# Three subtractions moved in an attention kernel: one within VectorE's order, two from VectorE to GpSimd

## The reference: a cross-attention transformer block

```python
h = _layernorm(x, ln1_g, ln1_b)
x = _attention(h, h, sa_wq, sa_wk, sa_wv, sa_wo, sa_bo) + x
h = _layernorm(x, ln2_g, ln2_b)
x = _attention(h, cond_emb, ca_wq, ca_wk, ca_wv, ca_wo, ca_bo) + x
h = _layernorm(x, ln3_g, ln3_b)
p = h @ ff_w1 + ff_b1
a, gate = (p[..., :D_FF], p[..., D_FF:])
h = a * jax.nn.gelu(gate, approximate=False) @ ff_w2 + ff_b2
return h + x
```

## Time and profile before

| what | before |
|---|---|
| median of three runs | 2842.57 us (2842.28 to 2843.34) |
| the profiled execution, its own time | 2842.41 us |
| its span in the profile | 2840.6 us |
| TensorE busy (matmul) | 2796.0 us, 98% |
| VectorE busy | 2262.0 us, 80% |
| ScalarE busy | 1910.5 us, 67% |
| GpSimd busy | 1468.7 us, 52% |

### The profile page before, as it was taken

One profiled execution on the slowest core, in us unless ns is written; L12 is line 12 of the kernel. 1 busy time (PEld: TensorE's weight loads), 2 busy tenths in 40 slices (PEclk: granted clock), 3 DMA queues, 4 the chain that ended last, 5 costly groups with the idle time before them and its releaser, 6 DMA issues.

```text
span 2840.6 us, 72796 instructions
## 1 busy us (share of the span) xinstructions
PE 2796.0 (98%) x25278; PEld 2490.1 (88%) x25278; DVE 2262.0 (80%) x3494; ACT 1910.5 (67%) x6043; POOL 1468.7 (52%) x1311
## 2 busy tenths in 40 slices
PE   8999999999999999999999999999999999999999
PEld 7888888888888888888888888888888889999999
DVE  7888888888888888888888888888888865555554
ACT  6777777777777777877777777777777754444443
POOL 5444444444444444755555555555555564554554
PEclk9999999999999999999999999999999999999999
DMA  6666666666666666767777776666666642222222
GB/s 158 151 160 161 162 161 162 162 154 153 155 153 153 151 153 153 179 166 173 172 173 172 171 171 164 164 164 164 165 164 163 149 101 86 80 74 82 84 74 64
DMA packets 355330, 413.33 MB, mean 146 GB/s; under 512 B 122017, under 2 KB 209441, under 8 KB 355233
## 3 DMA queue, kind: packets, MB, share of 16 engines
q1 hardware_dynamic: 345088, 395.29, 57.2%
q10 hardware_dynamic: 10144, 16.78, 1.6%
HBM read 94.52 MB, written 49.02 MB: 51 GB/s over the span
## 4 chain that ended last, share of the span: by engine, by line
PE 58%; issue 17%; POOL 12%; DVE 11%; ACT 1%; POOLq 0%; DMA 0%; DVEq 0%; ACTq 0%
PE unit_ps L629 31%; PE s_ps L629 12%; POOL probs L1357 10%; PE unit_ps L653 8%; PE s_ps L641 7%; DVE neg_max L1107 3%; DVE blocks L1121 2%; DVE hT_lo L1145 2%; DVE qk L1132 1%; POOL x_rb L1344 1%; ACT probs L911 1%; DVE row_blocks L1098 1%; POOL rstd L1336 1%; DVE a_lo L1127 0%; DVE hT_lo L1149 0%
## 5 line engine op out<-in xcount | busy, mean ns | idle before, releaser
L1357 POOL TENSOR_TENSOR probs<-probs,row_inv 128x1024 f32<-128x1024 f32 x512 | 972.6, 1900 | 1076.5 <-DVE row_inv L1112 1076.4
L911 ACT ACTIVATE probs<-s_ps,neg_max 128x256 f32<-128x256 f32 x2048 | 950.2, 486 | 508.7 <-DVE neg_max L1107 507.7
L1121 DVE STREAM_TRANSPOSE blocks<-probs 128x1024 f32<-128x1024 f32 x512 | 633.2, 1237 | 194.6 <-POOL probs L1357 194.6
L1107 DVE TENSOR_REDUCE neg_max<-s_ps 128x4 f32<-128x1024 f32 x512 | 611.5, 1195 | 5.6 <-PE s_ps L641 2.7
L629 PE MATMUL unit_ps<-hT_hi,w_hi 128*128 128x256 f32 x2048 | 580.0, 287 | 5.6 <-DVE hT_lo L1145 3.1
L629 PE MATMUL unit_ps<-hT_hi,w_lo 128*128 128x256 f32 x2048 | 555.1, 277 | 0.0
L629 PE MATMUL unit_ps<-hT_lo,w_hi 128*128 128x256 f32 x1792 | 497.3, 278 | 0.0
L653 PE MATMUL unit_ps<-pT,v_f 128*64 128x256 f32 x4096 | 456.6, 381 | 0.2 <-issue 0.2
L911 ACT ACTIVATION_READ_ACCUMULATOR probs<-s_ps,neg_max 128x1 f32 x2048 | 442.0, 216 | 0.0
L641 PEld LDWEIGHTS s_ps<-qk 64*128 64x128 f32 x6144 | 374.9, 185 | 70.6 <-issue 42.0
L641 PE MATMUL s_ps<-qk 64*128 64x256 f32 x6144 | 426.6, 284 | 5.9 <-ACT probs L911 5.4
(11 more groups left out here) (76 smaller groups left out, 4866.0 us busy)
## 6 DMA issues: line engine op xcount, KB each, us to landing
pT<-blocks SPq DMA_DIRECT2D x1024, 256.0 KB, 4.5
rows_t_dram<-row_blocks SPq DMA_DIRECT2D x91, 256.0 KB, 2.2
rows_in<-rows_t_dram SPq DMA_DIRECT2D x91, 256.0 KB, 4.4
x_res<-in_x_dram SPq DMA_DIRECT2D x32, 256.0 KB, 3.1
x_sa_dram<-x_out SPq DMA_DIRECT2D x32, 256.0 KB, 2.2
x_ln<-x_sa_dram ACTq DMA_DIRECT2D x32, 256.0 KB, 4.9
ctx_in<-in_ctx_dram SPq DMA_DIRECT2D x32, 256.0 KB, 4.1
x_res<-x_sa_dram SPq DMA_DIRECT2D x32, 256.0 KB, 2.8
```

The lines of the kernel that those rows point to most:

```text
L911: op = nc.scalar.activation(probs[:, m % 2, r, :].rearrange("p (j b c) -> p j b c", j=IT, c=BLK), scored.rearrange("p (j c b) -> p j b c", ...
L1107: nc.vector.tensor_reduce(neg_max[:, m % RING, :], s_ps[:, m % 2, :, :].rearrange("p h (i j) -> p (h i) j", j=S), AX_X, ALU.max, negate=Tr ...
L1121: nc.vector.transpose(blocks[:, n % 2, :, m % 2, :].rearrange("p b (j r c) -> p r j b c", j=IT, c=BLK), probs[:, m % 2, :, :].rearrange("p ...
L1357: nc.gpsimd.tensor_tensor(probs[:, m % 2, :, :], probs[:, m % 2, :, :], row_inv[:, m % RING, :].unsqueeze(2).broadcast_to([P, ROWS, S]), A ...
```

## The change

Three subtractions move; none is added or dropped.

1. VectorE's `attended_lo(t - 1, 3)`, the remainder of the fourth product with v, stood in step 2 behind the inverted sums of pair 4. It now stands behind the first maximum of the step (pair 4), ahead of the transpose of pair 3. This holds in self and in cross attention.
2. In cross attention, `x_remainder(t + 1)` leaves VectorE and is done by GpSimd, in step 2 behind the multiply of pair 5. In self attention it stays on VectorE in step 3.
3. `context_remainder(t + 1)` leaves VectorE's step 3 and is done by GpSimd, behind the rows' remainder and ahead of the 64x256 context subtraction that GpSimd had already.

```diff
-            def context_remainder(b):
-                dve.wait_ge(at.ctx_hi, b - ca.first + 1)
-                nc.vector.tensor_tensor(hT_lo[:, 1, 0, :], ctx_in[:, 0, :], f32(hT_hi[:, 1, 0, :]), ALU.subtract).then_inc(at.ctx_lo, 1)
-
...
                     if "cur" in parts:
                         maxima(t, 2 * n)
+                    if n == 2 and "prv" in parts:
+                        attended_lo(t - 1, 3)
                     if n == 0 and "prv" in parts:
                         qk_remainders(t, 2)
-                    if n == 3 and to_context:
-                        context_remainder(t + 1)
...
-                    if n == 2 and "prv" in parts:
-                        attended_lo(t - 1, 3)
...
-                    if n == 2 and "nxt" in parts and in_context:
-                        x_remainder(t + 1)
...
             def context_remainders(b):
                 c = b - ca.first
 
-                pool.wait_ge(at.norm_done, (b - 1) * PAIRS + 6)
                 pool.wait_ge(at.ctx_hi, c + 1)
+                nc.gpsimd.tensor_tensor(hT_lo[:, 1, 0, :], ctx_in[:, 0, :], f32(hT_hi[:, 1, 0, :]), ALU.subtract).then_inc(at.ctx_lo, 1)
+                pool.wait_ge(at.ctx_lo, 2 * c + 1)
                 nc.gpsimd.tensor_tensor(hT_hi[RIGHT, 1, 1, :], ctx_in[RIGHT, 1, :], f32(hT_hi[RIGHT, 1, 1, :]),
                                         ALU.subtract).then_inc(at.ctx_lo, 1)
                 pool.wait_ge(at.ctx_lo, 2 * c + 2)
+
+            def x_remainder(b):
+                pool.wait_ge(at.x_hi, b + 1)
+                nc.gpsimd.tensor_tensor(hT_lo[:, 0, :, :], hT[:], f32(hT_hi[:, 0, :, :]), ALU.subtract).then_inc(at.x_lo, 1)
...
                     if "cur" in parts:
                         normalise(t, 2 * n + 1)
+                    if n == 2 and "nxt" in parts and parts != FILL and pass_of(t, home).has_ctx:
+                        x_remainder(t + 1)
                     if n == 2 and "nxt" in parts and pass_of(t + 1, home).has_ctx:
                         context_remainders(t + 1)
```

More of the change, by code:

```diff
@@ L1218, in attention_iteration @@
                 in_context = parts != FILL and pass_of(t, home).has_ctx
-                to_context = "nxt" in parts and pass_of(t + 1, home).has_ctx
                 for n in range(STEPS):
```

## The result

The changed kernel takes 2870.03 us (median of four runs, 2869.48 to 2871.45), the kernel before 2842.66 in the same comparison. The ratio is 1.0097, with a 95% interval of 1.0079 to 1.0114: slower, by 27 us or 1.0%. The profiled execution took 2870.47 us, its span 2868.6.

A forecast was written before the change was run, and what follows sets the result against it. VectorE's work with GpSimd's multiplies was taken to bound cross attention at 35.28 us a batch; the change adds 1.32, of which 0.29 is swallowed and 1.03 shows, 32 us over 31 batches: 2874 us, range 2855 to 2886.

The forecast's parts named there:

- What bounds the kernel before: Cross attention: VectorE's work with GpSimd's multiplies between sets the 35.28 us period; TensorE follows with slack, needing about 34.3.
- Part 1: Fourth remainder moved up: +0.58 us a batch on VectorE and GpSimd's loop in cross attention, nothing in self attention.
- Part 2: Rows' remainder on GpSimd behind pair 5's multiply: 1.29 us, first query at 28.45, period 36.31 us in cross attention.
- the short one for v's bank: TensorE's wait ahead of the fourth v projection in cross attention: up to 0.6 us, ScalarE freeing the bank 0.58 us later.
- Part 3: Context's remainder on GpSimd: 0.75 us for each context subtraction, both done at 30.0, hidden by 0.6 us, costing nothing.
- the 6.85 us from the first query to the next scores: TensorE's 33 query and key matmuls plus 24 of output projection, without a gap, in cross attention: 6.85 us.
- What the old loop swallows: The route through the first query was 34.99 us, hidden under 35.28; of 1.32 us added, 0.29 is swallowed, 1.03 shows.
- A: VectorE's 2.27 us relief decides; cross attention runs at TensorE's 34.3 us a batch: 2812 us, chance 0.08.
- its break-even: How much earlier than worked out `x_lo` must come for the faster rival: break-even 1.03 us, the rival itself 2.0.
- B: No change: the moved fourth remainder's 0.58 us is absorbed and GpSimd's subtraction takes 0.69: 2842 us, chance 0.05.
- C: Only one of two terms, moved fourth remainder or slower GpSimd subtraction, is real: 14 us, 2856 us, chance 0.07.
- D: TensorE's longer gap in cross attention drops the granted clock once a batch, 2 us by 31: 2936 us, chance 0.05.

The follow-up runs named there:

- run 5: Kernel before with only the context's 128x256 remainder moved to GpSimd, the other two remainders staying on VectorE in their old places: 2833.49 us, ratio 0.9965.
- Run 1: Kernel before with only the fourth product's remainder moved up behind the step's first maximum, both other remainders staying on VectorE: 2861.66 us, ratio 1.0061.
- run 8: Changed kernel with one extra 128x512 GpSimd subtraction into an unread scratch tile, right ahead of the rows' remainder: 2914.32 us, ratio 1.0250.
- run 9: Changed kernel with one extra 128x512 GpSimd subtraction into an unread scratch tile, behind the context's remainders: 2870.57 us, ratio 1.0098.
- run 10: Changed kernel with the context's 128x256 remainder put back on VectorE: 2871.37 us, ratio 1.0099.
- run 7: Kernel before with only the rows' remainder moved, to GpSimd ahead of pair 5's multiply; the context's and fourth remainders stay on VectorE: 2825.12 us, ratio 0.9934.
- run 2: Changed kernel with the fourth product's remainder back in its old place; rows' and context's remainders on GpSimd: 2856.05 us, ratio 1.0042.

## Why the prediction was right

**What bounds the kernel before.** Right, and run 5 shows it: VectorE and GpSimd's loop, not TensorE, for all its 98%. The start of the scores tells the same: where VectorE waits for them, its first maximum follows 1.01 us later. Before the change it follows 1.30 us later and more in most batches, so VectorE was late; in the changed kernel it is 1.01 (1851.62 to 1852.63).

**Part 1.** Right within 0.03 us: forecast +0.58 us in VectorE's order, measured 0.60 (1835.28 to 1835.88), TensorE's stall gone, nothing won. The multiply of pair 5 starts 25.24 us behind the first maximum; the prediction had 25.21. Run 1 alone: 17.6 us in 31 batches, 0.57 us each. In self attention VectorE's wait for the rounded rows fell from 32.2 to 17.5 us in 25 batches, 0.59 us each, and TensorE stayed at 900.00 of 900.00: the cover was there.

**Part 2.** Right. `hT_lo` took 1.27 us on GpSimd (1.29 predicted), right behind the multiply, and the handover to TensorE 0.05 (0.10). TensorE's wait is 1.24 to 1.25 us where I had about 1.4, and the short one for v's bank is there, 0.35 us of idle matmul time. VectorE's wait on TensorE shows not at the first maximum, as forecast, but mainly at `x_out` right ahead of it (0.75 us). Runs 8 and 9 show that the place counts and not the load.

**Part 3.** Right in the changed kernel (run 10): both context subtractions took 0.74 us, and no wait for them is recorded. What the prediction did not say is that part 3 by itself would have been a gain.

**The term that was mis-sized** is the 6.85 us from the first query to the next scores. It measured 6.67 us in most batches of the changed kernel. I had read it from one batch, and that batch was one of five slower ones among 31. The next one of the kernel before:

```profile
1863.86 0.39 PE L629 MATMUL unit_ps<-hT_hi,w_hi 128*128 128x256 f32 x1
...
1870.55 0.62 PE L641 MATMUL s_ps<-qk 64*128 64x256 f32 x6
```

That is 6.69 us. With it the period would have come out at 36.15 and the time at 2869 us. The rest is small: 0.07 us less from handover and subtraction, 0.03 more up to the multiply. What the old loop swallows moved with the term, from 0.29 us to 0.45 in most batches (27.13 + 6.69 + 1.01 = 34.83, against 35.28), so 0.8 us a batch showed and not 1.03.

**The rivals.** A (VectorE's relief decides) did not happen, but its break-even did exist: in run 7 the rows' remainder comes ahead of the multiply, and the kernel is 18.6 us faster than before. B and C are excluded by runs 1 and 2, each of which costs something. D did not happen in the changed kernel, whose granted clock is 1.00 throughout cross attention; run 8 shows that it was one subtraction away.

## What to carry to other kernels

Before moving an instruction off a busy engine, write down the route from one iteration to the next through it, and through the engine that takes it over: here 2.3 us of relief on VectorE bought nothing, since the one consumer that was waiting got the result 1.3 us later, 0.7 by the change of engine and 0.6 by the multiply ahead of it, which part 1 had put off. An instruction that stands while its engine would wait anyhow is free; moved up to serve a visible stall, it can cost its full length on the loop that sets the period, and the stall it removes may be only slack of a follower. And a term of 57 instructions is worth reading in several iterations before it goes into a sum.

## What was not expected of the hardware

The same 57 matmuls between first query and next scores run at two speeds with the granted clock at 1.00 in both: in the kernel before, 6.69 us in one batch (1863.86 to 1870.55) and 6.85 in another (1828.58 to 1835.43), and 6.91 in run 2. The extra 0.2 us is spread over many matmuls, in the slower batch before over those of keys and output, in run 2 over the queries' too: their starts lie about 118 ns apart, otherwise 113. Some kernels are in the one or the other in all or nearly all batches, some change from batch to batch. No wait is recorded inside the stretch, and what sets it stays open; it was worth up to 0.24 us a batch, 7 us in all, which is more than this kernel's measurement tells apart.

The second is the clock. A stall of 1.25 us a batch (the changed kernel) left the granted clock at 1.00; with one of 2.47 us (run 8) it fell to 0.51 in four of 31 batches. The Trainium skill, "TensorE: Matmul & The Clock Gate", section "Why this matters for your kernels", says that idle gaps of the matmul engine bring the clock back to its lower level; the trace agrees in that the longer stall alone had such drops.
